# Graph attention on one core: four accumulator banks, one bank for the spread destinations, and another place for the spreads

## The reference

```python
h = (x @ W).reshape(N, HEADS, HEAD_DIM)
a_src = einsum('nhd,hd->nh', h, att_src)
a_dst = einsum('nhd,hd->nh', h, att_dst)
e = leaky_relu(a_src[src] + a_dst[dst], 0.2)
m = segment_max(e, dst)
e = exp(e - m[dst])
alpha = e / segment_sum(e, dst)[dst]
out = segment_sum(alpha * h[src], dst) + bias
```

## Time and profile before

| | |
|---|---|
| median of 3 runs | 4569.11 us (4560.88 to 4573.55) |
| the profiled execution | 4561.11 us, span 4559.4 us |
| mean granted TensorE clock | 0.81 of full speed |
| busy share of the span | PE 74%, DVE 59%, POOL 45%, ACT 34% |
| gathers of layer 0 to the last pair of transposes | 184.6 to 1388.5 us |
| the same of layer 1 | 2201.1 to 3404.0 us |
| emptying of the pipeline | to 1427.7 us and to 3432.4 us |

### The profile page before, as it was taken

The page is one execution under the profiler, slowest core; times in us unless marked ns, Lnnn a source line. Parts: engine busy times, 40 slices in busy tenths (PEclk is TensorE's granted clock), DMA queues, the critical chain, the costliest instruction groups (busy, mean ns, idle before and its releaser), DMA issues. The chain is left out here.

```text
span 4559.4 us, 73301 instructions
## 1 busy us (share of the span) xinstructions
PE 3353.3 (74%) x16240; PEld 2520.2 (55%) x16241; DVE 2681.5 (59%) x8451; ACT 1561.4 (34%) x4383; POOL 2064.2 (45%) x2095
## 2 busy tenths in 40 slices
PE   5267766676666788856366666666658999999999
PEld 3144444444444577744244444444437888888888
DVE  7489999999987855546356565665655422222221
ACT  2133334333332123322233333333333433333333
POOL 0277777777770033348577777777750000000000
PEclk9677777777876579977677777777778999999999
DMA  3344444444453134434344444444461000000000
GB/s 100 81 104 107 107 106 106 106 107 107 108 98 87 34 122 157 160 89 126 87 105 105 106 105 106 105 106 106 106 78 59 7 5 7 4 7 7 4 7 7
DMA packets 382578, 369.58 MB, mean 81 GB/s; under 512 B 249324, under 2 KB 309388, under 8 KB 382242
## 3 DMA queue, kind: packets, MB, share of 16 engines
q0 software_dynamic: 107072, 272.84, 24.1%
q1 hardware_dynamic: 272774, 92.39, 8.5%
q10 hardware_dynamic: 2396, 0.84, 0.1%
HBM read 324.13 MB, written 41.59 MB: 80 GB/s over the span
## 5 line engine op out<-in xcount | busy, mean ns | idle before, releaser
L684 POOL DMA_INDIRECT g_G<-rows,g_pack x1856 | 1811.2, 976 | 784.3 <-issue 478.3
L717 PE MATMUL bank<-g_G,g_MB 128*125 128x260 f32 x1856 | 661.7, 503 | 213.6 <-DVE acc L923 212.1
L923 DVE SCALAR_TENSOR_TENSOR acc<-acc,g_c,bank 125x65 f32 (+1 forms) x2320 | 617.5, 314 | 148.6 <-PE bank L717 75.4
L717 PE MATMUL bank<-g_G,g_M 128*125 128x257 f32 x1856 | 634.6, 490 | 20.4 <-DVE acc L923 20.3
L1364 DVE SCALAR_TENSOR_TENSOR X<-bank,e_cw,X 125x256 f32 (+1 forms) x400 | 175.1, 479 | 793.7 <-PE bank L1190 793.7
L717 PEld LDWEIGHTS bank<-g_G,g_MB 128*125 128x125 f32 x1856 | 421.6, 245 | 357.0 <-DVE acc L923 248.2
L1260 ACT ACTIVATE e_h<-bank,e_bi_c,e_sc_c 128x250 f32<-128x250 f32 x800 | 404.2, 556 | 557.8 <-PE bank L1181 420.3
L788 ACT ACTIVATE g_mt_d<-bank,unode 125x256 bf16<-125x256 f32 x928 | 383.3, 463 | 453.9 <-PE bank L702 453.3
L717 PEld LDWEIGHTS bank<-g_G,g_M 128*125 128x125 f32 x1856 | 419.1, 242 | 147.0 <-DVE acc L923 25.7
L1190 PE MATMUL bank<-e_w,e_h 128*125 128x256 f32 x1600 | 379.2, 380 | 3.1 <-ACT e_h L1260 3.1
L1181 PE MATMUL bank<-e_h,e_w 128*128 128x250 f32 x1600 | 375.9, 377 | 1.2 <-ACT e_h L1260 1.2
(11 more groups left out here) (302 smaller groups left out, 4168.6 us busy)
## 6 DMA issues: line engine op xcount, KB each, us to landing
g_G<-rows,g_pack POOLq DMA_INDIRECT x1856
acc<-in_edge_attr SPq DMA_DIRECT2D x50, 531.2 KB
g_pack<-edge_pack SPq DMA_DIRECT2D x928, 2.0 KB
g_drow<-edge_dst SPq DMA_DIRECT2D x928, 1.0 KB
expert_out<-x_y SPq DMA_DIRECT2D x54, 256.0 KB
g_qe<-edge_q SPq DMA_DIRECT2D x464, 1.0 KB
rows<-acc SPq DMA_DIRECT2D x25, 253.9 KB
rows<-n_T SPq DMA_DIRECT2D x25, 251.0 KB
```

Of the source, the lines that this page charges most:

```text
L684: nc.gpsimd.indirect_dma_start(G[:, r, q, :], None, rows_d[l], bass.IndirectOffsetOnAxis(ap=pack[:, r, q, 0:1], axis=0)).then_inc(S(p + f" ...
L717: mm_ = nc.tensor.matmul(sum_bank(r, k, u)[0:TN, 0:HW], left, G[:, rk, q, :], start=(c == 0), stop=(c == C - 1))
L923: ins = nc.vector.scalar_tensor_tensor(at, at, c1[:, rk, u, h:h + 1], sum_bank(r, k, u)[0:TN, h * W:(h + 1) * W], ALU.mult, ALU.add)
```

## The change

There are four sum banks, 4, 5, 1 and 7, taken by the number of the unit in its slot; a sum waits for `merge` of the unit four before it in place of three. `w_ps` moves from bank 7 to bank 3. All spreads go to bank 2, so each spread but the first few waits for `mt_abs` of the one before it, that is for `place` of the pair ahead. Spread 0 moves ahead by two sums (behind `sums(3, 4)`), spread 2 by one (ahead of `sums(2, 1)`). No instruction is added or taken away, and the order on ScalarE, VectorE, GpSimd and SyncE stays.

```diff
-            w_ps = bank[7][:, 0:QH].rearrange("p (q h) -> p q h", h=H)
+            w_ps = bank[3][:, 0:QH].rearrange("p (q h) -> p q h", h=H)
-            def sum_bank(r, k, u):
-                return bank[(4, 5, 1)[((r - k) % RING * U + u) % 3]]
+            def sum_bank(u):
+                return bank[(4, 5, 1, 7)[u % 4]]
 ...
-                            if v_ >= 2 or late(i, 2):
-                                after(pe, p + "mt_abs", i * V - V + (v_ - 1))
-                            nc.tensor.matmul(bank[2 + v_ % 2][0:TN, :], ...
+                            if v_ >= 1 or late(i, 2):
+                                after(pe, p + "mt_abs", i * V - V + v_)
+                            nc.tensor.matmul(bank[2][0:TN, :], ...
 ...
-                            if u >= 3 or late(i, k + 1):
-                                after(pe, p + "acc", i * U - k * U + (u - 2))
+                            if u >= 4 or late(i, k + 1):
+                                after(pe, p + "acc", i * U - k * U + (u - 3))
 ...
                         sums(3, U - 4)
+                        spread(0)
                         sums(3, U - 3)
                         sums(3, U - 2)
-                        spread(0)
                         spread(1)
                         sums(3, U - 1)
 ...
+                        spread(2)
                         sums(2, 1)
-                        spread(2)
                         spread(3)
                         sums(2, 2)
```

More of the change, by code:

```diff
@@ L699, in spread @@
                                 pe.wait_ge(S(p + f"drow_in{r1}"), filled(t, r, 1, 16 * U))
-                            if v_ >= 2 or late(i, 2):
-                                after(pe, p + "mt_abs", i * V - V + (v_ - 1))
-                            nc.tensor.matmul(bank[2 + v_ % 2][0:TN, :], ones_bf[:, :], drow[:, 2 * v_:2 * v_ + 2, :].rearrange("k u e -> k (u e)"),
+                            if v_ >= 1 or late(i, 2):
+                                after(pe, p + "mt_abs", i * V - V + v_)
+                            nc.tensor.matmul(bank[2][0:TN, :], ones_bf[:, :], drow[:, 2 * v_:2 * v_ + 2, :].rearrange("k u e -> k (u e)"),
                                              start=True, stop=True).then_inc(S(p + "spread"), 1)
@@ L716, in sums @@
                                 left = MB[:, rk, q, :] if l == 0 else M[:, turn(r, k, u // 2), q % CP, :]
-                                mm_ = nc.tensor.matmul(sum_bank(r, k, u)[0:TN, 0:HW], left, G[:, rk, q, :], start=(c == 0), stop=(c == C - 1))
+                                mm_ = nc.tensor.matmul(sum_bank(u)[0:TN, 0:HW], left, G[:, rk, q, :], start=(c == 0), stop=(c == C - 1))
                             mm_.then_inc(S(p + "summed"), 1)
@@ L788, in place @@
                                 ins = nc.scalar.activation(mt_d[:, v_ % 2, k * C:(k + 1) * C, :],
-                                                           bank[2 + v_ % 2][0:TN, k * UE:(k + 1) * UE].rearrange("p (e c) -> p c e", c=C), ACT.Abs,
+                                                           bank[2][0:TN, k * UE:(k + 1) * UE].rearrange("p (e c) -> p c e", c=C), ACT.Abs,
                                                            bias=unode[0:TN, bass.ds(i * U - U + (2 * v_ + k), 1)])
@@ L915, in merge @@
                                 at = acc[:, bass.ds(j * HW, HW)]
-                                ins = nc.vector.tensor_tensor(at, at, sum_bank(r, k, u)[0:TN, 0:HW], ALU.add)
+                                ins = nc.vector.tensor_tensor(at, at, sum_bank(u)[0:TN, 0:HW], ALU.add)
                             else:
@@ L922, in merge @@
                                     at = acc[:, bass.ds(j * HW + h * W, W)]
-                                    ins = nc.vector.scalar_tensor_tensor(at, at, c1[:, rk, u, h:h + 1], sum_bank(r, k, u)[0:TN, h * W:(h + 1) * W],
+                                    ins = nc.vector.scalar_tensor_tensor(at, at, c1[:, rk, u, h:h + 1], sum_bank(u)[0:TN, h * W:(h + 1) * W],
                                                                          ALU.mult, ALU.add)
```

## The result

| | before | after |
|---|---|---|
| median | 4570.97 us (4558.06 to 4576.47, 12 runs) | 4581.17 us (4573.50 to 4590.31, 12 runs) |
| ratio | | 1.0027, 95% interval 1.0016 to 1.0038 |
| span of the profiled execution | 4559.4 us | 4578.9 us |
| mean granted TensorE clock | 0.81 | 0.76 |

The forecast was 4567 us and no change, with 4538 to 4598 us as the range. The time lies in that range, but it did move, and the slower rival (4587 us) is nearer to it than the forecast. In the experiments, one execution of g (11,996 us) and one of h (7571 us) lie far outside all others; the ratios leave them out, and the medians count them.

The account below looks back on a forecast made before the run. Gathers on POOL, partly held by VectorE, were taken to bound both attentions. Layer 1's +9, layer 0's -8 and the emptying's -1 us sum to 0; from the 4566 us mean it predicted 4567 us, range 4538 to 4598.

Parts of the forecast that it names:

- the slower rival: Layer 1's incidences move into two gathers' starts, 0.8 us a slot held; layer 0 at 0.5; 4587 us; chance 0.29.
- The gathers bound both attentions and VectorE's incidences hold them: Both layers: undisturbed slots of 20.03 us, 58 making 1162 of 1204 us; VectorE's holds add 0.48 and 0.44 a slot.
- Four banks and the spreads' waits cost nothing themselves: TensorE: removed merge waits (1.57 us a layer 0 slot) are worth nothing by themselves; early spread waits cost nothing.
- Layer 0 falls out of step with POOL and waits for the rows: Layer 0: VectorE's slot drops from 20.30 to 19.76 us, under POOL's 20.03, so it waits for rows.
- Laying gathers 1.252 us apart against them gives ... mean 0.34: Layer 0: incidences starting at 17.2 to 18.1 us hold gathers 0.34 us a slot on the mean, against 0.48.
- -8 us: Layer 0's term: held time changes by -0.14 us in each of 58 slots; ends -28 and +10 us.
- the 0.48 us: Layer 0 before the change: the stretching of gathers per slot beyond their median of 0.947 us.
- VectorE's 0.54 us of waiting: Layer 0: waiting for line 1006 within VectorE's 20.30 us slot, 0.54 us, which the change was to remove.
- TensorE's work ahead of line 743 is the same, so it stays at 6.64 us: Layer 1: line 743 stays at 6.64 us after the slot's first transpose; line 1006 moves from 7.90 to 7.25.
- +9 us: Layer 1's term: held time goes from 0.44 to 0.60 us in each of 58 slots; ends -5 and +27 us.

Follow-up runs that it names:

- g: The changed kernel with 12 unused TensorE products ahead of line 766 and 3 at the slot's end; 4581.17 us, 1.0030 of the kernel before.
- h: The changed kernel with the ramp that line 956 compares kept in PSUM, f32 instead of bf16; 4540.17 us, 0.9938 of the kernel before.
- f: The changed kernel with its spreads in their old places, 20.5 us slots; 4582.45 us, 1.0034 of the kernel before.
- o: The kernel before with line 956's ramp in PSUM, 25 us slots; 5156.78 us, 0.9975 of the kernel before.
- q: The kernel before with line 956's ramp in PSUM, sought at 20.5 but run at 25 us slots; 5127.90 us, 0.9967 of the kernel before.
- r: The kernel before with line 956's ramp in PSUM, once more, again at 25 us slots; 5168.78 us, 0.9989 of the kernel before.
- p: The kernel before with one added VectorE reduction ahead of layer 0's first incidence, 20.5 us slots; 4584.93 us, 1.0041 of the kernel before.
- b: The changed kernel (four sum banks, one spread bank) with spreads in their old places, 25 us slots; 5098.20 us, 0.9895 of the kernel before.
- c: The kernel before with the two spreads moved and nothing else, 25 us slots; 5160.32 us, 1.0018 of the kernel before.

## Why the prediction was wrong, step by step

- *The gathers bound both attentions and VectorE's incidences hold them*: right for the kernel before. Line 684's time and the whole time changed together, +20.0 and +19.5 us, and h, which takes the hold away, gives back 45 us. The prediction named this as its test. In the changed kernel it is right for layer 0; in layer 1 only 15 of 55 slots still wait for rows. Line 969, which the prediction also has as a holder, only prolongs a hold, in layer 0. The Trainium skill ("SBUF — State Buffer", section "Who interferes with whom") says that VectorE contends with a GpSimd operation that reads SBUF when both of its own inputs are in SBUF, and not with one such input at most. h agrees: with one of the two inputs in PSUM all gathers are free. The same section says that issue order decides who blocks. The rows show nearly nothing of that the other way round: the pair at 639.03 starts 0.26 us into a gather and takes its usual 1.26 us, and only an incidence that starts within 0.03 us of a gather is longer, by 0.03 to 0.07 us.
- *Four banks and the spreads' waits cost nothing themselves*: nothing speaks against it, and it is not shown. The waits for merges went, and the places of the spreads do not matter (f). The runs that were to measure the rest (o, q and r) fell on chips with 25 us slots.
- *"Layer 0 falls out of step with POOL and waits for the rows"*: right. Line 731 waits for its rows 83.1 us between 300 and 1340 us where it waited 28.7.
- *"Laying gathers 1.252 us apart against them gives ... mean 0.34"*: the step that failed. It gave -8 us, and the gathers of layer 0 took 20.4 us more: 0.82 us held a slot where 0.34 was put. It laid the gathers on a fixed grid. But a held gather moves the grid: the next starts 1.12 us behind the end of the incidence that held it, and the next incidence starts 0.69 us behind that end, so a slot is held two or three times in a row. Held time is then 0.23 us plus the phase: never under 0.23, and about 0.85 as the mean of a whole step. The place was wrong too: the incidences stood 19 to 20.7 us behind line 731, not 17.2 to 18.1. That matters less, since almost any place costs more than before's.
- The deeper fault is in what I took the 0.48 us for. I read it as what chance gives and looked for shifts around it. It was the cheap end: the earlier trace rows has held gathers 20.30 us apart and a first incidence of 0.72 us, which is one that starts together with a gather, at phase 0.0. Leaving that place could only cost. I had seen that VectorE's 0.54 us of waiting belonged to it, and counted the loss of the step as a gain. Why the old timing stays at 0.0 in 34 of 50 slots and the new one at no phase is open; p shows only that a delay loses it as well.
- *Layer 1: "TensorE's work ahead of line 743 is the same, so it stays at 6.64 us"*: wrong, without effect. Line 743 comes 8.4 us behind line 731 on the mean (6.5 before) and line 1006 at 9.0, not 7.25. TensorE works at 1.2 GHz for most of the layer (granted 0.60): a spread takes 0.68 us and four sum matmuls 2.08, where 0.42 and 1.13 are had at 2.4 GHz. +9 us were forecast, and the gathers of the layer took 0.5 us less. That the new place costs the same is luck: nothing in the working gives it. The prediction also has no sign of the ring that h shows.
- The rival on the slower side had the right sign, in the wrong layer: layer 1 at 0.8 us a slot and layer 0 at 0.5. It was the other way round.

## What to carry to other kernels

Where two engines disturb each other periodically, find the phase of each slot before forecasting: tabulate the cost by phase, and ask whether the kernel sits at the cheap end. If it does, a change of either engine's timing, a faster one too, can cost as much as the mean over phases; the change and the delay p both did. Better than tuning the phase is to take the disturbance away: moving one operand of line 956 to PSUM, at no cost in its duration, made the changed kernel 1% faster (4540.17 us) and faster than the kernel before by 0.6%. When the held time went, a ring through TensorE and VectorE was the next bound in layer 1, at 20.47 us a slot where the gathers alone need 20.03.

## What the runs showed of the hardware

- The same kernel takes about 4565 us on some chips and 5145 to 5173 us on others, and edits can differ in sign between them: one and the same kernel is 0.34% slower (f) and 1.05% faster (b) than the kernel before. On the slower chips all engines stop together, for about 2 us (c, o, r), once in one or two slots.
- A gather of 0.947 us that starts while VectorE runs line 956 with both operands in SBUF ends no sooner than 0.82 us after that line's end. One that starts within 0.03 us of the line's start is not always held. With one operand in PSUM the same operation, as long, holds none of 1856.
- The hold is one-sided: among 2784 incidences in six traces, only those that start within 0.03 us of a gather are longer than 0.69 us (0.74 at most).
- More work on TensorE raised its granted clock from 0.76 to 0.85 over the kernel (g against the changed kernel), and its added products cost no time at 20.5 us slots (4581.17 against 4584.91 us).
